# Layer 1's expert results: each in a place of its own in DRAM, added after reading back, in place of scatters that add in DRAM

## What is computed

```
masked = where(emask > 0, sigmoid(logits) + bias, -inf)
_, topidx = top_k(masked, 6)                      # six of 32 experts for each token
eo     = (silu(x @ w_gate[e]) * (x @ w_up[e])) @ w_down[e]
routed = sum over the token's six experts of weight * eo
anchor = one of 16 small experts, chosen by topidx[:, 0] // 2
out    = x + routed + shared + 0.1 * anchor
```

## Time and profile before

| what | value |
|---|---|
| median of 3 runs | 1102.74 us (1100.43 to 1111.35) |
| the profiled execution's own time | 1102.11 us |
| its span, first to last instruction | 1100.4 us |
| PE busy | 938.3 us (85%) |
| DVE busy | 643.0 us (58%) |
| POOL busy | 612.7 us (56%) |
| ACT busy | 474.8 us (43%) |
| mean granted TensorE clock | 0.873 of full speed |

### The profile page before, as it was taken

One profiled execution on the slowest core, in us unless ns is written; L12 is line 12 of the kernel. 1 busy time (PEld: TensorE's weight loads), 2 busy tenths in 40 slices (PEclk: granted clock), 3 DMA queues, 4 the chain that ended last, 5 costly groups with the idle time before them and its releaser, 6 DMA issues. The chain is left out here.

```text
span 1100.4 us, 23121 instructions
## 1 busy us (share of the span) xinstructions
PE 938.3 (85%) x6360; PEld 687.4 (62%) x6360; DVE 643.0 (58%) x3193; ACT 474.8 (43%) x1594; POOL 612.7 (56%) x529
## 2 busy tenths in 40 slices
PE   5988888766899999879997998858699999999980
PEld 2666656544468889557765766644587767777750
DVE  3676666444245455346866766657465656565548
ACT  2776566533123343327645454221154544444430
POOL 1015555555617777693143434546588888888861
PEclk9898888666899999989969767568899999999985
DMA  9997511001679997660011241275799998888888
GB/s 330 345 374 270 174 51 48 33 19 40 224 212 315 320 317 124 124 199 32 23 63 61 74 168 64 79 298 224 232 185 254 217 154 147 155 152 158 147 233 314
DMA packets 133712, 191.19 MB, mean 174 GB/s; under 512 B 17988, under 2 KB 111117, under 8 KB 132562
## 3 DMA queue, kind: packets, MB, share of 16 engines
q1 hardware_dynamic: 85234, 126.74, 35.5%
q0 software_dynamic: 41280, 54.57, 25.2%
q10 hardware_dynamic: 7072, 8.40, 2.3%
HBM read 101.14 MB, written 99.77 MB: 183 GB/s over the span
## 5 line engine op out<-in xcount | busy, mean ns | idle before, releaser
L988 POOL DMA_INDIRECT buf<-R,RI x240 | 234.9, 979 | 330.0 <-ACT R L1150 153.6
L1036 POOL DMA_INDIRECT yb<-YT,DI x98 | 151.4, 1545 | 64.7 <-DVE DI L1610 40.0
L773 PE MATMUL PS<-R,XT 128*128 x632 | 152.1, 364 | 0.0
L317 PE MATMUL PS<-R 128*128 128x256 f32 (+2 forms) x352 | 125.1, 490 | 13.1 <-DMA R<-in_ctxT 10.0
L1618 DVE COPY XT<-PS 128x256 f32<-128x256 f32 x222 | 93.7, 422 | 35.0 <-PE PS L322 20.3
L773 PEld LDWEIGHTS PS<-R,XT 128*128 128x128 f32 x632 | 104.6, 194 | 7.5 <-issue 0.7
L1036 POOL DMA_INDIRECT yb<-AS_,DI x62 | 95.9, 1546 | 18.9 <-issue 11.6
L317 PEld LDWEIGHTS PS<-R 128*128 128x128 f32 (+1 forms) x352 | 72.6, 226 | 48.0 <-issue 36.6
L789 PE MATMUL PS<-R,AT 128*128 (+1 forms) x316 | 101.5, 404 | 0.0
L1907 DVE TENSOR_TENSOR AC<-SL,PS 128x128 f32<-128x128 f32 (+1 forms) x158 | 43.2, 273 | 89.2 <-ACT SL L1325 59.5
L1150 ACT ACTIVATE R<-R,MX 128x120 f32<-128x120 f32 x256 | 80.0, 387 | 34.3 <-DVE MX L1440 27.3
(11 more groups left out here) (209 smaller groups left out, 1897.6 us busy)
## 6 DMA issues: line engine op xcount, KB each, us to landing
R<-in_ew SPq DMA_DIRECT2D x64, 384.0 KB
BX<-buf SPq DMA_DIRECT2D x128, 140.0 KB
yb<-Z SPq DMA_DIRECT2D x34, 512.0 KB
R<-buf SPq DMA_DIRECT2D x94, 140.0 KB
R<-in_w SPq DMA_DIRECT2D x8, 1536.0 KB, 21.5
buf<-Z SPq DMA_DIRECT2D x8, 1120.0 KB, 13.3
R<-yb SPq DMA_DIRECT2D x16, 512.0 KB, 3.5
R<-yb SPq DMA_DIRECT2D x8, 1024.0 KB, 16.9
```

The costliest lines, as they stand in the source:

```text
L317: m = e.matmul(out_, left, right, start=(i == 0), stop=(i == len(pairs) - 1))
L773: x = e.matmul(PS[:, 2 + j % 2, 0:2 * wd], XT[:, j % 3, k, :], src[:, bass.ds(regs[j], 1), k * 2 * wd:(k + 1) * 2 * wd].rearrange("p a n - ...
L988: e.indirect_dma_start(out=(buf1 if l else buf0)[:, :], out_offset=bass.IndirectOffsetOnAxis(ap=RI[:, n % 6, k:k + 1].bitcast(U32), axis=0 ...
L1036: e.indirect_dma_start(out=yb[:, :], out_offset=bass.IndirectOffsetOnAxis(ap=DI[:, j:j + 1].bitcast(U32), axis=0), in_=(YTS0 if i < E0 els ...
```

## The change

Layer 1's results no longer add in DRAM. `yb1` has six rows for each token, one for each of its six experts, and the row's number comes from constants (`d1` is 6 times the token plus the rank). All of layer 1's tiles go through `put_back`. DVE's `yf_add` now sums six rows for each token instead of four, one group of 128 tokens at a time (16 calls), and the first calls stand inside the loop: position 152 to 160 run `yf_add(0)` to `yf_add(8)`, after the work on the tile of that position. Each load of `yb1` grows from 1 MiB to 1.5 MiB. The zeroing of `yb1`, its semaphore and the waits on it go. Layer 0 keeps its adding scatters.

```diff
-        ("d1", (np.where(k < 6, t * Q, t) - OFF).reshape(P, -1)),
+        ("d1", (np.where(k < 6, t * 6 + k, t) - OFF).reshape(P, -1)),
...
-    yb1 = nc.dram_tensor("yb1", [(2048 + P) * Q, D], F32)
+    yb1 = nc.dram_tensor("yb1", [2048 * 6, D], F32)
...
-        YF = R[:, 0:NT * Q * D].rearrange("p (s n) -> p s n", s=NT)
+        YF = R[:, 0:NT * 1536].rearrange("p (s n) -> p s n", s=NT)
...
-                    e.dma_start(y1f[:, rs, :], Z[:, 0:D].unsqueeze(1).broadcast_to([P, 4, D])).then_inc(S["z_y1"], 16)
...
-            def put_back(i):
+            def put_back(i, yb, bound):
                 w.wait_ge("a_yt", i + 1)
                 w.wait_ge("d_di", i + 1)
                 e.indirect_dma_start(
-                    out=yba[:, :], out_offset=bass.IndirectOffsetOnAxis(ap=DI[:, i - E0:i - E0 + 1].bitcast(U32), axis=0),
-                    in_=YTS[result(i)[0]], in_offset=None, bounds_check=2047, oob_is_err=False).then_inc(
+                    out=yb[:, :], out_offset=bass.IndirectOffsetOnAxis(ap=DI[:, i - E0:i - E0 + 1].bitcast(U32), axis=0),
+                    in_=YTS[result(i)[0]], in_offset=None, bounds_check=bound, oob_is_err=False).then_inc(
                         S[f"yt{result(i)[0]}"], 16)
...
-            w.wait_ge("z_y1", 16 * 17)
             for i in range(NTL):
-                if ORDER[i] < T1:
-                    add_back(E0 + i, yb1, E0 + ORDER.index(ORDER[i] - Q) if ORDER[i] >= Q else None)
-                else:
-                    put_back(E0 + i)
+                yb, bound = (yb1, 2048 * 6 - 1) if ORDER[i] < T1 else (yba, 2047)
+                put_back(E0 + i, yb, bound)
...
-            def yf_add(g):
-                ns = slice(2 * g, 2 * g + 2)
-                w.wait_ge(f"w1_{g}", 32)
-                e.tensor_tensor(YF[:, ns, 0:512], YF[:, ns, 0:512], YF[:, ns, 512:1024], ALU.add).then_inc(*dv.up())
+            def yf_add(n):
+                yl = YF[:, n, :]
+                w.wait_ge(f"w1_{n // 2}", 32)
+                e.tensor_tensor(yl[:, 0:768], yl[:, 0:768], yl[:, 768:1536], ALU.add).then_inc(*dv.up())
+                t = dv.n
+                w.wait_ge("dv", t)
+                w.wait_ge("d_add", 32)
+                e.tensor_tensor(X[:, n, :], X[:, n, :], yl[:, 512:768], ALU.add).then_inc(*dv.up())
+                e.tensor_tensor(yl[:, 0:256], yl[:, 0:256], yl[:, 256:512], ALU.add).then_inc(*dv.up())
                 w.wait_ge("dv", dv.n)
-                w.wait_ge("d_add", 32)
-                e.tensor_tensor(X[:, ns, :], X[:, ns, :], YF[:, ns, 256:512], ALU.add).then_inc(*dv.up())
-                w.wait_ge("dv", dv.n)
-                e.tensor_tensor(X[:, ns, :], X[:, ns, :], YF[:, ns, 0:256], ALU.add).then_inc(S["d_xf"], 1)
+                e.tensor_tensor(X[:, n, :], X[:, n, :], yl[:, 0:256], ALU.add).then_inc(S["d_xf"], 1)
...
-                    matches(E0 + i, TE[:, ORDER[i]:ORDER[i] + 1], ORDER[i] % Q if ORDER[i] < T1 else None)
+                    matches(E0 + i, TE[:, ORDER[i]:ORDER[i] + 1], None)
...
-            for g in range(NB):
-                yf_add(g)
+                if ROUTED + 6 <= i:
+                    yf_add(i - ROUTED - 6)
+            for n in range(NTL + 3 - ROUTED - 6, NT):
+                yf_add(n)
```

More of the change, by code:

```diff
@@ L133 @@
     + [f"l_x{i}" for i in range(4)] + ["l_" + n for n in WNAMES]
-    + [f"sc{i}" for i in range(6)] + ["z_b0", "z_y0", "z_y1", "z_dum"]
+    + [f"sc{i}" for i in range(6)] + ["z_b0", "z_y0", "z_dum"]
     + [f"ew{i}" for i in range(NEW // 2)] + [f"bx{i}" for i in range(NBX)] + [f"yt{i}" for i in range(NYT)]
@@ L288, in build @@
         yv0 = yb0.rearrange("(t k) d -> t (k d)", k=Q)
-        yv1 = yb1.rearrange("(t k) d -> t (k d)", k=Q)
+        yv1 = yb1.rearrange("(t k) d -> t (k d)", k=6)
         yv1p = yv1.rearrange("(n p) m -> p n m", p=P)
@@ L800, in clears @@
                 b0f = buf0.rearrange("a b -> (a b)").rearrange("(p r n) -> p r n", p=P, n=ROW)
-                y0f, y1f = (y.rearrange("a b -> (a b)").rearrange("(p r n) -> p r n", p=P, n=D) for y in (yb0, yb1))
+                y0f = yb0.rearrange("a b -> (a b)").rearrange("(p r n) -> p r n", p=P, n=D)
                 for r in range(0, 64, 8):
@@ L1023, in put_back, with add_back @@
                 e.indirect_dma_start(
-                    out=yba[:, :], out_offset=bass.IndirectOffsetOnAxis(ap=DI[:, i - E0:i - E0 + 1].bitcast(U32), axis=0),
-                    in_=YTS[result(i)[0]], in_offset=None, bounds_check=2047, oob_is_err=False).then_inc(
+                    out=yb[:, :], out_offset=bass.IndirectOffsetOnAxis(ap=DI[:, i - E0:i - E0 + 1].bitcast(U32), axis=0),
+                    in_=YTS[result(i)[0]], in_offset=None, bounds_check=bound, oob_is_err=False).then_inc(
                         S[f"yt{result(i)[0]}"], 16)
-            def add_back(i, yb, same):
+            def add_back(i):
                 w.wait_ge("a_yt", i + 1)
                 w.wait_ge("d_di", i + 1)
-                if same is not None:
-                    slot, n = result(same)
+                if i >= Q:
+                    slot, n = result(i - Q)
                     w.wait_ge(f"yt{slot}", 16 * n)
-                j = i if i < E0 else i - E0
                 e.indirect_dma_start(
-                    out=yb[:, :], out_offset=bass.IndirectOffsetOnAxis(ap=DI[:, j:j + 1].bitcast(U32), axis=0),
-                    in_=(YTS0 if i < E0 else YTS)[result(i)[0]], in_offset=None, bounds_check=(2048 + P) * Q - 1,
+                    out=yb0[:, :], out_offset=bass.IndirectOffsetOnAxis(ap=DI[:, i:i + 1].bitcast(U32), axis=0),
+                    in_=YTS0[result(i)[0]], in_offset=None, bounds_check=(2048 + P) * Q - 1,
                     oob_is_err=True, compute_op=ALU.add).then_inc(S[f"yt{result(i)[0]}"], 16)
@@ L1042, in _ @@
             for i in range(E0):
-                add_back(i, yb0, i - Q if i >= Q else None)
+                add_back(i)
             def y_add():
@@ L1913, in _ @@
                 w.wait_ge(f"ya{g}", 16)
-                w.wait_ge("d_xf", 2 * g + 2)
+                w.wait_ge("d_xf", 4 * g + 4)
                 e.tensor_tensor(X[:, ns, :], X[:, ns, :], YA[:, ns, :], ALU.add).then_inc(S["d_out"], 1)
```

## The result

The changed kernel takes 1123.18 us (median of 4 executions, 1121.12 to 1132.16); the kernel before, run beside it, 1107.05 us. The ratio is 1.0176 (95% interval 1.0130 to 1.0222): 1.8% slower, where I had predicted 0.9% faster and a range of 1086 to 1105. The ratio is taken from executions in the same, faster state of the chip, so it is not the quotient of the two medians, 1.0146. So the change costs 1 to 2%.

A forecast was written before the change was run, and what follows sets the result against it. POOL's scatters were taken to bound layer 1's loop, and read-back, DVE's additions and output the end. Terms -2.0 - 16.5 + 8.3 = -10.2 us gave 1091.9 against the profiled 1102.1, so a 1092.6 median; range 1086 to 1105.

The forecast's parts named there:

- Step 1: Layer 1's scatters on POOL: 127 turn from adding to plain, 1.0 + 0.3 = 1.3 us each, under PE's 1.63.
- Rival D: POOL's scatter time belongs to the 128 rows, not the addition, so the loop keeps 1.84 us; 1118.5 us, chance 0.07.
- Step 2: Layer 1 positions 0 to 53: ACT's lateness from waiting for scatters goes; gain 2 us, bounds 0 and 6.1.
- Rival B: Positions 0 to 53 give back all 6.1 us, as ACT's lateness began with waits for landings; 1088.5 us, chance 0.15.
- Step 3: Layer 1 positions 54 to 144: PE becomes the limit, 142.9 us against 159.4; gain 16.5 us.
- the sum's -10.2: Whole kernel: predicted net change in us, from -2.0 and -16.5 in the loop and +8.3 in the tail.
- step 8: Layer 0: removing 17 zeroing DMAs costed at nothing, with 2 us of gain as the other bound.
- Rival E: Layer 1 loop: something else, ACT's jobs or tile loads, holds 1.75 us per position; 1111 us, chance 0.07.
- Steps 4 to 7: From position 145 to the end: read-back start, larger loads, DVE's new wait and its additions; tail 8.3 us longer.
- T: Time of position 145's transposes, from which the tail is measured; before the change the span ended 59.6 us later.
- Rival C: Read-back: loads share DMA engines, first group lands 17 us after issue, DVE waits 10 more; 1102.6 us, chance 0.15.

The follow-up runs named there:

- e7: Changed kernel with layer 1's routed results sent by direct transfers of 128 consecutive rows instead of indirect scatters; 1.3% faster than the kernel before.
- e3: Kernel before with layer 1's scatters writing instead of adding, all else kept; positions 54 to 145 took 164.3 us, 5 more than before.
- e6: Changed kernel with three small fills on POOL, and a wait for each, behind every routed scatter of layer 1; positions 54 to 145 took 189 us.
- e4: Changed kernel with the 17 removed zeroing DMAs put back on a scratch tensor, and DVE's wait for them; median of all ten executions 1113.4 us.
- e1: Changed kernel with all 16 of layer 1's row-group adds placed behind the loop again; 1113.1 us.
- e2: Changed kernel with unused rows of a tile written to spare rows instead of being dropped by the bounds; 1112.3 us.
- e9 to e12: Changed kernel with, per routed scatter, one waited fill; that plus adds behind the loop; a wait for the landing two positions earlier; two waited fills. None faster.
- e17: The kernel before, unedited, run again for a second profile; positions 54 to 145 took 158.9 us.

## Why the prediction was wrong

**Step 1 (POOL's scatters) was right.** 973 ns against the 1.0 us taken; starts 1.28 us apart at the closest. POOL's lag behind PE was 8.3 us at position 0 and 8.8 at position 54 (15.1 before), later up to 11.5. Rival D fell.

**Step 2 (positions 0 to 53)**: a gain of 2 forecast. The first profile shows a loss of 0.5; over the ten profiles with plain scatters and no binding wait it is 89.4 to 94.6, with a mean of 91.8. That is 2.3 less than the 94.1 before, so the 2 us agree, as far as one profile before and a spread of 5 us let this be said. Rival B's 6.1 did not come.

**Step 3 failed**, and it is 25.3 of the 31.0 us between the sum's -10.2 and the 20.8 measured (step 8 adds 4.7, step 2 2.5, and the tail gives 1.5 back): "142.9 us against 159.4. Gain 16.5, if PE becomes the limit", with "nothing else in the loop gets work". The measured stretch is 168.2, and 161 to 167 in its repeats and in the variants without a binding wait. The forecast for step 3 took PE's undisturbed pace from positions in which POOL was not yet the limit, and took for granted that a POOL that is done sooner disturbs nobody. With direct transfers PE comes close to that pace: 149.1 us, 10.3 of the 16.5. Of the other 6, 3.7 are a mis-sized pace (the median start of a routed position is 1.68 us behind the one ahead in 14 of the 19 profiles, e7's among them, not 1.63, times 73). What turned the 10 us of gain into a loss of 2 to 9 are late starts of DVE and ACT, on results that PE has long had ready. They come with plain indirect scatters that follow one another closely: in the kernel before with the addition taken out they are there (e3, 24), with direct transfers (e7) and with plain scatters 2.2 us apart (e6) they are gone. The price of step 3 is thus 12 to 19 us above what the direct transfer shows.

Rival E had this outcome as seen from outside, "routed positions at 1.75 us with POOL idle", but I gave it 0.07, and its mechanism (ACT's jobs or tile loads) was another: the tile loads land some 5 us or more ahead of their transposes. Rival D's 1118.5 came nearest to the first result, by a mechanism that step 1 excludes. My argument against E, that PE had held 1.63 us in the same loop, was read from stretches in which POOL issued adding scatters.

**Steps 4 to 7 (the tail) were right**, by mechanism and nearly by size. With T = 1054.81: first the chain that ended last, then DVE's timeline, both of the changed kernel (start us, us, what):

```profile
1063.92 2.79 DMA yb<-YT,DI
1066.79 6.89 DMA R<-yb
1073.70 0.97 DVE R L1883
...
1114.30 2.27 DVE X L1913 x2
```

```profile
1069.11 0.21 DVE L1903 TENSOR_TENSOR AC<-SL,PS 128x64 f32<-128x64 f32 x1
1073.70 0.96 DVE L1883 TENSOR_TENSOR R<-R 128x768 f32<-128x768 f32 x1 [4.38 <-DMA R<-yb]
```

Read-back begins at T + 12.0 (forecast 10.8), the first group lands 6.9 us after its issue (7.0), DVE waits from T + 14.5 to T + 18.9 (12.4 to 17.8) and ends at T + 61.8 (63.2), the span at T + 66.4 (67.9). The tail is 6.8 us longer, where 8.3 was forecast. In the repeats it is 66.0 to 66.8. Rival C fell.

**Step 8 (layer 0 at nothing)**: position 0 came 4.7 us later in the first comparison, and e4, which brings the zeroing back, has it later still. This varies by as much between profiles of the same kind. Shown is only that no gain or loss above that can be seen.

What stays open: by what path plain scatters hold up the sequencers of SP, and DVE's and ACT's starts; whether it is their distance, how many are in work, or in part their kind (the adding scatter never came closer than 1.84 us to another adding one); whether a distance of 1.5 us without a wait would do; why two chips show no hold-up, and whether the change gains there what was predicted, since the changed kernel did not run on them. Nor did any kernel with indirect scatters, on a chip with the hold-up, have both no late starts and a POOL that is not the limit, so that their removal alone gives back the 10 us is argued from e7, not shown. What the runs settle is the place, in this order: not the adds, rows or zeroing (e1, e2, e4), the change from adding to plain scatters (e3), their being indirect (e7), and how closely POOL issues them (e6).

## What to carry to other kernels

An engine that is taken off the critical path also stops pacing the others. Before counting its time as a gain, look for a stretch of the trace in which it already ran as it will after the change, with the same kind of instruction beside it; a pace that was read where another kind was issued is no evidence. And when a release brings nothing, look at the plainest instructions of an engine with no part in it: a register move that goes from 29 to 700 ns says that the hold-up is shared. An edit that makes a symptom go away shows nothing unless the unedited kernel has the symptom on the same chip; where it did not run there, look in the trace for code that all kernels share. Last, a wait for an instruction on the same engine has its own price, 0.6 us here for a fill of 0.13.

## What the runs showed of the hardware

- On POOL an indirect scatter of 128 rows of 1 KB takes 973 ns without and 1546 ns with the addition, a direct transfer of the same rows 542 ns. The next one starts 0.3 us after the end of each.
- On four chips plain indirect scatters issued behind one another at 1.28 us delay others: SP's register moves go from 29 to 729 ns, DVE's copies start up to 2 us late. With direct transfers (e7) or with plain scatters 2.2 us apart (e6) no copy is late, and none with adding scatters at 1.84 us. On two other chips (e9 to e12, e17) no such delay shows, even beside plain scatters at 1.28 us.
- A fill of 0.13 us on POOL and a wait for it move the next scatter from 1.28 to 1.87 us behind the last; the same fill without the wait leaves it at 1.27.
- DVE's addition of 768 elements with both inputs in SBUF takes 955 ns alone and 1570 ns beside POOL's additions.
